# A bidirectional Mamba block with a quantized linear layer on one core: a re-joined order of the engines' lists, an earlier start, no Relu pass, and eight batches written out

## The reference

```python
xz = einsum('ed,bld->bel', in_proj_w, xn)            # x: 256 rows, z: 256 rows
def mamba_dir(xz, ...):                              # forward, and on the time-reversed sequence
    u = silu(causal_conv(x, conv_w, 4 taps) + bias)
    x_dbl = einsum('bdl,kd->bkl', u, xproj_w)        # 8 rows for delta, 16 B, 16 C
    delta = softplus(dtproj_w @ x_dbl[:, :8] + dt_bias)
    h[t] = exp(delta[t] * A) * h[t-1] + delta[t] * B[t] * u[t]     # 256 channels x 16 states
    y = sum_n(h * C) + D * u
    return y * silu(z)
mamba = out_proj_w @ (out_f + reversed(out_b))
xh = xn @ Hadamard; s = max(max|xh| over channels, 1e-5) / 7
ffn = (clip(round(xh / s), -8, 7) * s) @ ternary(weight).T
```

## Time and profile before

| | |
|---|---|
| median of 3 runs | 982.82 us (979.82 to 986.75) |
| the profiled execution | 989.38 us |
| its span | 987.6 us |
| PE busy | 802.9 us (81%) |
| DVE busy | 787.0 us (80%) |
| POOL busy | 788.1 us (80%) |
| ACT busy | 780.7 us (79%) |
| mean granted TensorE clock | 0.875 |
| DMA | 72.44 MB, 73 GB/s |

### The profile page before, as it was taken

The page is one execution under the profiler, slowest core; times in us unless marked ns, Lnnn a source line. Parts: engine busy times, 40 slices in busy tenths (PEclk is TensorE's granted clock), DMA queues, the critical chain, the costliest instruction groups (busy, mean ns, idle before and its releaser), DMA issues.

```text
span 987.6 us, 13840 instructions
## 1 busy us (share of the span) xinstructions
PE 802.9 (81%) x3873; PEld 381.5 (39%) x3873; DVE 787.0 (80%) x795; ACT 780.7 (79%) x1452; POOL 788.1 (80%) x493
## 2 busy tenths in 40 slices
PE   2478887979888897888889797897978889797974
PEld 1134434343443434333353434434343343434352
DVE  2248887988888888888789887888978887988982
ACT  2469896988959887798869889698887988699950
POOL 1038978997899887898789977989879897798994
PEclk9677998899998989889879989889898898898796
DMA  3070607051160605215070421607043150704300
GB/s 86 11 162 29 135 4 182 3 123 41 57 136 3 159 3 124 68 53 107 3 170 24 115 44 39 154 3 159 3 104 88 33 129 3 169 15 99 61 22 11
DMA packets 50841, 72.44 MB, mean 73 GB/s; under 512 B 6128, under 2 KB 19328, under 8 KB 50816
## 3 DMA queue, kind: packets, MB, share of 16 engines
q1 hardware_dynamic: 50384, 71.87, 31.3%
q10 hardware_dynamic: 432, 0.26, 0.1%
HBM read 60.58 MB, written 11.53 MB: 73 GB/s over the span
## 4 chain that ended last, share of the span: by engine, by line
POOL 33%; issue 32%; ACT 13%; PE 11%; DVE 7%; SPq 1%; DMA 1%; POOLq 1%; DVEq 0%; ACTq 0%
POOL hst L612 22%; ACT da L370 5%; POOL dbx_t L622 5%; DVE hst L512 4%; PE pb L744 3%; ACT dbx_t L359 3%; POOL t_log L628 3%; PE b_ps L827 2%; PE b_ps L824 2%; POOL xn L674 2%; DVE b_ps L500 1%; PE pb L751 1%; PE y L841 1%; DMA rep<-d_scr 1%; PE pb L771 1%
## 5 line engine op out<-in xcount | busy, mean ns | idle before, releaser
L612 POOL TENSOR_TENSOR hst<-hst,c_rep 128x1024 f32<-128x1024 f32 x256 | 601.4, 2365 | 132.2 <-DVE hst L512 128.4
L512 DVE TENSOR_TENSOR_SCAN hst<-da,b_ps 128x512 f32<-128x512 f32 x512 | 589.5, 1203 | 82.1 <-ACT da L370 43.4
L827 PE MATMUL b_ps<-ident,dbx_t 128*128 128x128 f32 x1536 | 241.9, 298 | 127.3 <-DVE hst L512 120.1
L370 ACT ACTIVATE da<-rep,neg_a 128x511 f32<-128x511 f32 x512 | 335.6, 709 | 6.4 <-DMA rep<-d_scr 6.3
L827 PEld LDWEIGHTS b_ps<-ident,dbx_t 128*128 128x128 f32 x1536 | 178.2, 150 | 277.5 <-DVE hst L512 230.1
L359 ACT ACTIVATE dbx_t<-du_t,b_t 128x256 f32<-128x256 f32 x576 | 248.1, 495 | 2.9 <-PE b_ps L827 2.9
L841 PE MATMUL y<-hst,sum_sel 128*32 128x512 f32 x1024 | 166.6, 730 | 0.0
L744 PE MATMUL pb<-xnt,conv_wt 128*128 128x512 f32 x256 | 120.7, 616 | 0.7 <-ACT xnt L291 0.7
L824 PE MATMUL b_ps<-t_log,spread_sel 32*128 32x512 f32 x256 | 89.3, 698 | 10.6 <-DVE hst L512 10.6
L500 DVE TENSOR_TENSOR b_ps<-b_ps,b_rep 128x1024 f32<-128x1024 f32 x64 | 78.1, 1220 | 21.6 <-PE b_ps L824 21.6
L622 POOL TENSOR_TENSOR dbx_t<-du_t,b_t 128x1024 f32<-128x1024 f32 x48 | 91.2, 1901 | 2.7 <-ACT du_t L342 2.7
(11 more groups left out here) (90 smaller groups left out, 598.5 us busy)
## 6 DMA issues: line engine op xcount, KB each, us to landing
rep<-d_scr SPq DMA_DIRECT2D x128, 256.0 KB, 9.3
c_rep<-bc_scr SPq DMA_DIRECT2D x64, 256.0 KB, 5.0
d_scr<-t_pos SPq DMA_DIRECT2D x16, 512.0 KB, 3.0
b_rep<-bc_scr SPq DMA_DIRECT2D x64, 64.0 KB, 2.4
x_ln<-x SPq DMA_DIRECT2D x8, 256.0 KB, 3.2
x_res<-x SPq DMA_DIRECT2D x8, 256.0 KB, 2.9
out<-x_res SPq DMA_DIRECT2D x8, 256.0 KB, 9.5
conv_wt<-conv_w SPq DMA_DIRECT2D x2, 512.0 KB, 5.9
```

Of the source, the lines that this page charges most:

```text
L370: nc.scalar.activation(da[s % 2][:, j, 1:L], rep[d][h][:, j, 1:L], ACT.Exp, scale=neg_a[:, d, h, j, q:q + 1]).then_inc(decay_done, 1)
L512: nc.vector.tensor_tensor_scan(hst[s % RING][:, j, :], da[s % 2][:, j, :], b_ps[:, j, :], 0.0, ALU.mult, ALU.add).then_inc(scan_done, 1)
L612: nc.gpsimd.tensor_tensor(hst[s % RING][:, two, :], hst[s % RING][:, two, :], c_rep[d][:, q:q + 1, :].broadcast_to([P, 2, L]), ALU.mult).t ...
L827: ins = tr(b_ps[:, j, P * c:P * (c + 1)], dbx_t[(NX * d + q - 1) % 2][:, c, NJ * h + j, :, :].rearrange("p r e -> p (r e)"), ident[:, :])
```

## The change

- Loop: `batches` calls body(b) for all eight b, so every wait is for a constant.
- Relu: the dt bias becomes a row of the dt matmul (a row of ones is made in xdbl by the bias operand of `keep_xdbl`); L327 goes; 1 + exp goes to t_pos instead of pb, the two corrections of `log1p` run in t_pos with t_log and t_exp (all in SBUF), and the last step takes max(pb, 0) minus it, in one instruction.
- Quantizer: clip and rescaling move from POOL to DVE, in `quantize`, rounding and clip in place in pb; PE's wait for had_read becomes one for xq_ready.
- Lists: ACT's decays and inputs_t stand in another order with u_sigmoid, xdbl, xnt, normalize and keep_dut, mostly half a slot to a slot later; DVE's times_b stands a step ahead of its scan; POOL's refine goes from slot 3 to 4; PE's convs of U + 2 stand both in slot 7, around the second half of the next unit's first inputs.
- Start: the normalization goes ahead of ACT's wait for the weights; the first conv goes ahead of the ternary weight's transpose, which goes to y; the dt matmuls go ahead of b's transposes; the first softplus and du run half by half; SP loads B and C of the first unit before delta, and delta's first half alone. Two more small loads (dt_bias).

```diff
 def batches(eng, body):
-    body(0)
-    with eng.Fori(1, NB - 1) as i:
-        body(i)
-    body(NB - 1)
+    for b in range(NB):
+        body(b)
...
 # SP, first unit
-            spread(0, 0)
+            store_bc(0, 0)
+            load_bc(0, 0)
+            sp.wait_ge(first_delta, 1)
+            sp.dma_start(d_scr[0][0], t_pos[:, 0, :]).then_inc(first_stored, DMA)
+            sp.wait_ge(first_stored, DMA)
+            load_delta(0, 0)
+            sp.wait_ge(delta_ready, 1)
+            sp.dma_start(d_scr[0][1], t_pos[:, 1, :]).then_inc(delta_stored, DMA)
+            sp.wait_ge(delta_stored, DMA)
+            load_delta(0, 1)
...
 # ACT, softplus
-                    nc.scalar.activation(t_exp[:, h, :], pb[:, h, :], ACT.Abs, bias=col[:, d, 1, h:h + 1]).then_inc(sp_step, 1)
-                    nc.scalar.activation(t_pos[:, h, :], pb[:, h, :], ACT.Relu, bias=col[:, d, 1, h:h + 1]).then_inc(sp_step, 1)
+                    nc.scalar.activation(t_exp[:, h, :], pb[:, h, :], ACT.Abs).then_inc(sp_step, 1)
...
-                nc.scalar.activation(pb[:, :, :], t_exp[:, :, :], ACT.Copy, bias=1.0).then_inc(sp_step, 1)
+                nc.scalar.activation(t_pos[:, :, :], t_exp[:, :, :], ACT.Copy, bias=1.0).then_inc(sp_step, 1)
...
 # ACT, start
-            act.wait_ge(w_loaded, DMA * W_LOADS)
-            nc.scalar.activation(neg_a[:, :, :, :, :], neg_a[:, :, :, :, :], ACT.Exp).then_inc(a_exp, 1)
             log_var(0)
             guess_rstd(0)
             normalize(0)
             keep_xnt(0)
+            act.wait_ge(w_loaded, DMA * W_LOADS)
+            nc.scalar.activation(neg_a[:, :, :, :, :], neg_a[:, :, :, :, :], ACT.Exp).then_inc(a_exp, 1)
...
 # ACT, unit (the new list)
+                    decays(b, d, s, 0)
+                    if s == 0:
+                        if d == 0 and not first(b):
+                            keep_dut(d, U, 1)
+                        inputs_t(d, U, 1, 1)
+                    if s == 1:
+                        inputs_t(d, U, 1, 3)
+                        if nxt:
+                            u_sigmoid(e, V, 1)
+                    if s == 2:
+                        if nxt:
+                            keep_xdbl(e, V)
+                        if d == 0 and not first(b):
+                            keep_xqt(b - 1)
+                        inputs_t(d, U, 2, 2)
...
+                    if s == 6 and d == 0 and not last(b):
+                        normalize(b + 1)
+                    if s == 7 and d == 0:
+                        if not last(b):
+                            keep_xnt(b + 1)
+                        keep_dut(e, V, 0)
+                    decays(b, d, s, 1)
+                    if s == 0:
+                        inputs_t(d, U, 1, 2)
+                        if nxt:
+                            u_sigmoid(e, V, 0)
+                    if s == 1:
+                        inputs_t(d, U, 2, 0)
+                        inputs_t(d, U, 2, 1)
+                    if s == 2:
+                        inputs_t(d, U, 2, 3)
+                        if nxt:
+                            keep_bt(e, V)
+                            softplus_in(e, V)
...
+                    if s == 7 and nxt:
+                        keep_dut(e, V, 1 - d)
+                        inputs_t(e, V, 1, 0)
...
 # DVE
-                    ins = nc.vector.tensor_scalar(xq[:, c, :], pb[:, 0, P * c:P * (c + 1)], qinv[:, c:c + 1], ROUND, ALU.mult, ALU.add)
-                ins.then_inc(had_read, 1)
+                    at = slice(P * c, P * (c + 1))
+                    ins = nc.vector.tensor_scalar(pb[:, 0, at], pb[:, 0, at], qinv[:, c:c + 1], ROUND, ALU.mult, ALU.add)
+                ins.then_inc(xq_step, 1)
+                dve.wait_ge(xq_step, 2 * b + 1)
+                nc.vector.tensor_scalar(pb[:, 0, :], pb[:, 0, :], ROUND, Q_POS, ALU.subtract, ALU.min).then_inc(xq_step, 1)
+                dve.wait_ge(xq_step, 2 * b + 2)
+                for c in range(NC):
+                    ins = nc.vector.tensor_scalar(xq[:, c, :], pb[:, 0, P * c:P * (c + 1)], -Q_NEG, qscale[:, c:c + 1], ALU.max, ALU.mult)
+                ins.then_inc(xq_ready, 1)
...
-                nc.vector.scalar_tensor_tensor(pb[:, :, :], pb[:, :, :], 1.0, t_log[:, :, :], ALU.subtract, ALU.subtract).then_inc(cor_step, 1)
+                nc.vector.scalar_tensor_tensor(t_pos[:, :, :], t_pos[:, :, :], 1.0, t_log[:, :, :], ALU.subtract, ALU.subtract).then_inc(cor_step, 1)
...
-                nc.vector.tensor_tensor(t_pos[:, :, :], t_pos[:, :, :], pb[:, :, :], ALU.subtract).then_inc(delta_ready, 1)
+                nc.vector.scalar_tensor_tensor(t_pos[:, :, :], pb[:, :, :], 0.0, t_pos[:, :, :], ALU.max, ALU.subtract).then_inc(delta_ready, 1)
...
+                    if s == 0:
+                        times_b(b, d, 0, 0)
                     scan(b, d, s, 0)
+                    if s < NH:
+                        times_b(b, d, s, 1)
...
                     scan(b, d, s, 1)
+                    if s < NH - 1:
+                        times_b(b, d, s + 1, 0)
...
 # PE, unit
                     if s == 7 and not last(b):
                         if d == 0:
-                            conv(d, U + 2, 1, range(TAPS), dut_ready, 2 * V + 2)
-                        else:
-                            conv(d, U + 2, 0, range(TAPS), dut_ready, 2 * V + 1)
+                            pe.wait_ge(xnt_ready, b + 2)
+                        conv(d, U + 2, 0, range(TAPS), dut_ready, 2 * V + 1)
                     next_inputs(s, 1)
...
-                    if s == 7 and d == 1 and not last(b):
+                    if s == 7 and not last(b):
                         conv(d, U + 2, 1, range(TAPS), dut_ready, 2 * V + 2)
```

More of the change, by code:

```diff
@@ L28 @@
 XC = 64
+ONE = DR + 2 * NS
 RING = 4
@@ L32, with build @@
 NX = NQ - 1
-def build(nc, x, win_t, wz_t, conv_w, cols, xproj_t, dt_t, a_log, wout_t, ffn_w, had, ident_d, sum_sel_d, spread_d, out):
+def build(nc, x, win_t, wz_t, conv_w, cols, xproj_t, dt_t, dt_bias, a_log, wout_t, ffn_w, had, ident_d, sum_sel_d, spread_d, out):
     ctx = ExitStack()
@@ L312, in keep_xdbl @@
                 wait(act, bc_stored, DMA * V - DMA)
-                nc.scalar.activation(xdbl[d][0:XC, :], pb[0:XC, 1, :], ACT.Copy).then_inc(xdbl_ready, 1)
+                nc.scalar.activation(xdbl[d][0:XC, :], pb[0:XC, 1, :], ACT.Identity, bias=ident[0:XC, ONE:ONE + 1]).then_inc(xdbl_ready, 1)
             def keep_bt(d, V):
@@ L387, in _ @@
             inputs_t(0, 0, 1, 0)
-            inputs_t(0, 0, 1, 1)
             def unit(b, d):
@@ L661, in scales @@
                 nc.gpsimd.tensor_scalar(qscale[:, :], amax[:, :], Q_FLOOR, 1.0 / Q_POS, ALU.max, ALU.mult).then_inc(q_step, 1)
-            def had_free(b):
-                pool.wait_ge(had_read, b + 1)
-            def clip(b):
-                nc.gpsimd.tensor_scalar(xq[:, :, :], xq[:, :, :], ROUND, Q_POS, ALU.subtract, ALU.min).then_inc(q_step, 1)
-            def clipped(b):
-                pool.wait_ge(q_step, 2 * b + 2)
-            def rescale(b):
-                for c in range(NC):
-                    ins = nc.gpsimd.tensor_scalar(xq[:, c, :], xq[:, c, :], -Q_NEG, qscale[:, c:c + 1], ALU.max, ALU.mult)
-                ins.then_inc(xq_ready, 1)
             for n, value in enumerate((0.25, 1.5, 0.5)):
@@ L710, in unit @@
                         inputs_t(e, 1)
-                    if s == 7 and d == 1:
-                        clip(b)
-                        clipped(b)
                     if s == 5 and d == 1:
@@ L718, in unit @@
                         scales(b)
-                    if s == 7 and d == 1:
-                        rescale(b)
                     if d == 0 and not last(b):
@@ L810, in project, with copies @@
                     ins.then_inc(out_filled, 1)
+            def copies(S, h, p):
+                for j in (2 * p, 2 * p + 1):
+                    at = slice(CB * j, CB * (j + 1))
+                    wait(pe, scan_done, NJ * (S - 1) + j + 1)
+                    mm(b_ps[:, j, :], spread_sel[at, :], du[at, h, :], start=True, stop=True).then_inc(t_filled, 1)
             def inputs(b, d, s, p):
@@ L816, in inputs @@
                     pe.wait_ge(du_ready, 2 * b + d + 1)
-                elif h == 0 and p == 0:
+                    copies(S, h, p)
+                    return
+                if h == 0 and p == 0:
                     pe.wait_ge(bm_act, NX * (2 * b + d) + q)
@@ L821, in inputs @@
                     wait(pe, scan_done, NJ * (S - 1) + j + 1)
[L822 to L827 removed]
+                    for c in range(NC):
+                        ins = tr(b_ps[:, j, P * c:P * (c + 1)], dbx_t[(NX * d + q - 1) % 2][:, c, NJ * h + j, :, :].rearrange("p r e -> p (r e)"), ident[:, :])
                     ins.then_inc(t_filled, 1)
@@ L847, in _ @@
             transpose_xn(0, xn_ready, 1)
+            pe.wait_ge(weights_ready, 2)
+            pe.wait_ge(xnt_ready, 1)
+            conv(0, 0, 0, range(TAPS), xnt_ready, 1)
+            conv(0, 0, 1, range(TAPS), xnt_ready, 1)
```

(21 more changed lines are left out.)

166 lines of the change are left out of this document (89 added, 77 removed).

## The result

The changed kernel takes 999.51 us (median of 4 runs, 998.43 to 1001.17) against 981.32 for the kernel before on the same chip: **1.0181 times the time before, 95% interval 1.013 to 1.0232**. The change is a loss of 18 us where a gain of 49 was forecast (982.8 to 934). The profiled execution has a span of 997.0 us.

What follows compares the result with a forecast made beforehand. Four in-order engine lists holding each other up, followed on DVE, were taken as the bound. Start-up 49, batch 0 107.75, six batches 666.6, batch 7 and end 115, plus 1.8 gave 940.2, scaled to 934 us; range 900 to 964.

Steps and rivals of the forecast that it cites:

- The correction in SBUF: Logarithm's corrections on DVE: two SBUF inputs may wait for GpSimd; +2.4 us a batch, ends 0 and 9.5.
- Rival C: DVE's corrections pay the wait for GpSimd in full, delaying its products: up to +12 us a batch, 1030; chance 0.06.
- ACT's list: ACT's reordered list in a looped batch: DVE's waits for decays fall from 6.9 to 0.5 us, -6.4.
- rival B: Waits only move: half the 8.3 us from ACT's list and Relu returns as PE waits, 967 us; chance 0.22.
- Early products and convs: PE's convs and early products with B make slot 1's inputs 1.4 us late, twice a batch: +2.8.
- the gain of 2.1: DVE's 4.3 us of waits for PE's scan inputs, put on PE's lower clock, halve with shorter gaps: -2.1 a batch.
- Loop: -1.4: Without the loop, register arithmetic showing between product and scan on DVE goes: -1.4 us a looped batch.
- rival D: Unrolling does nothing, all register work being hidden: 8 us less gain, inside the range; chance counted within the forecast's 0.52.
- Relu: -1.9: Two Relu passes a unit leave ACT; DVE's waits for the logarithm fall from 2.7 to about 0.8 us a batch.
- Quantization: +1.9: Clip and rescaling come from POOL to DVE's list, with no cover: +1.9 us a batch.
- Start-up 49: Time to the first decay falls from 62.9 to 49 us by earlier normalization, delta by halves and earlier loads; ends 47 and 52.
- end -6.3: Behind the last scan, POOL's last product and the last sum come sooner without POOL's clip and rescaling: -6.3 us.

Runs made afterwards that it cites:

- after: The changed kernel, with all parts of the change, against the kernel before: 999.51 us, 1.0181 times the time before.
- e1: Changed kernel with the logarithm's corrections regrouped so each has one operand in PSUM, clamp of the rounding error left out: 953.26 us.
- e5: Changed kernel with the regrouped corrections of e1 and the products with B back ahead of their own scans: 931.52 us.
- e13: e5 with ACT's list of a unit and POOL's refine slot as before the change: 959.4 us.
- e14: e13 with PE's two convs of d = 0 also back in slots 6 and 7: 957.77 us.
- e3: Changed kernel with the product with B put back directly ahead of its own scan: 980.43 us.
- e4: Changed kernel with the loop over batches 1 to 6 put back: 1000.63 us.
- e11: Kernel before the change with all eight batches written out, nothing else changed: 972.0 us.
- e10: e5 with the loop over batches 1 to 6 put back: 953.34 us.
- e12: e5 with the Relu pass back for all units but the first, and the corrections in pb: 948.44 us.
- e9: e5 with the quantizer's clip and rescaling back on POOL: 942.66 us.
- e2: Changed kernel with the Relu pass back for all units but the first, and the corrections in pb: 963.57 us.
- e8: Kernel before the change with only 1 + exp and the two corrections moved to SBUF, Relu pass kept: 1018.34 us.

## Why the prediction was wrong

The forecast for the profiled execution was 940.2, and it took 998.8. Of these 58.6 us, 49.9 are in batches 1 to 6 (28.2 less was forecast, 21.7 more came), 7.2 in batch 0 (-3.3, +3.9) and 2.2 in batch 7 with the end (-3.9, -1.7; there too the sum counted four corrections, and the batch has two). The other 7 of the whole error (999.5 - 934 = 65.5) come from the scaling by 0.66%, which the changed kernel's execution didn't follow. A middle batch was forecast at 111.35 us and takes 119.1, 7.75 more; the forecast's own sign of being wrong, a batch at 115 or more, was met.

- *The correction in SBUF: the step that failed most.* "+2.4 ... I take a quarter" of four whole products. The mechanism was named and the Trainium skill's rule spoke for it; the size was off. It costs 6.6 a batch (after against e1), **4.2 more** than the term. The reason given for a quarter, that POOL has gaps and that the first of a pair can start as its scan ends, doesn't hold at this place: POOL's dbx_t starts right as its product ends, and in all 15 pairs both corrections meet POOL. Rival C had this mechanism at up to 12 a batch and the wrong side from 6 over the term; by the 46 us of e1, 4.2 alone would have left a gain (an estimate: 934 + 34 = 968).
- *ACT's list: -6.4 was taken, 3.3 to 3.5 a batch was there* (e5 against e13 and e14): **2.9 more**. The waits for decays did go as forecast (6.9 to 0.8 a batch). From e13 to e5 they fall by 37.1 us in all, and nearly half of that comes back: 13.2 at u, for ACT's own gates, and 4.3 for PE. This was rival B, near its size (2.9 of its 4.15), but mostly for ACT where B had said PE. And the term was put on the list alone, where the time of a run shows a gain only together with the convs in slot 7 (2.7 and 3.2 in the shortest batches).
- *Early products and convs: +2.8 was taken*, for "1.4 late, twice a batch". The product with B waits five times a batch, and its early place costs 3.2 us in a middle batch (119.1 to 115.9 from after to e3; 112.5 to 109.25 from e1 to e5): **0.4 more**. The size was right and the cause half: the order on DVE carries it all, since the convs' pair, left in place in e3 and e5, is no loss there. Of the gain of 2.1 that was taken for PE's own waits, the 4.3 before show 3.3 after. The reading behind it was half right: the wait of 2.4 in the earlier trace rows ends a stretch at the lower clock (0.50 from 423.3 to 430.0), the one of 1.9 in the earlier trace rows comes at the higher (1.00 from 478.0 to 494.9).
- *Loop: -1.4*: nothing in after (e4), 1.6 a looped batch in the kernel before (e11, 9.6 us), 3.6 in e5 (e10). Right for the kernel before, wrong for this one, where another wait stood in its place: rival D held here, at 8 us.
- *Relu: -1.9*: the number is right (2.1 in e12 against e5), the way to it is not: DVE's waits for the logarithm hardly differ (13.4 and 14.9 us in all), so that it fits is in part luck. *Quantization: +1.9*: right in busy time (1.8), but the time of batches 1 to 6 doesn't show it (e9).
- *Start-up 49 and end -6.3*: right, 48.45 and -7.5, each link of the start-up within half a microsecond.

The terms 4.2, 2.9, 0.4 and the loop's 1.4 give 8.9 for the 7.75 that are to be explained. They are taken partly in e5 and partly in after, and those from whole runs hold a share of long batches, so the sum closes only to about a microsecond a batch. The 4.2 is measured by e1, and e2 and e8 show its cause.

The forecast's method had the flaw behind these: it added up waits removed one at a time, from a trace in which four engines hold each other up. Here the waits inside the two corrections came in full, and of the waits for decays that were removed nearly half came back. For TensorE's clock it took half of 4.3 us; between two batches of e5 a lower clock goes with 6.6.
